# Marking the closing branch at the head of every paired loop of a four-layer graph kernel

## What is computed

```python
# layer 0: masked attention with 8 heads of 64
atts = einsum('hqk,hmk->hqm', x@Wq, x@Wk) / 8 - 1e16 * (1 - adj_or_eye)
out0 = einsum('hqm,hmk,hko->qo', softmax(atts), x@Wv, Wo)
# layer 1: relu((adj @ x) @ W.T + b)
# layer 2: edge attention; h = x @ edge_w; e = where(adj > 0, h @ h.T, -9e15)
out2 = adj * (softmax(x@node_w, axis=0) * softmax(e, axis=1)) @ (x@weight) + bias
# layer 3: relu((D^-1/2 (adj+I) D^-1/2 @ x) @ W.T + b)
```

## Time and profile before

| | us |
|---|---|
| median of three runs | 2666.68 |
| lowest, highest | 2665.36, 2668.89 |
| span of the profiled execution | 2664.4 |
| TensorE busy in it | 2511.2 |
| VectorE, ScalarE, GpSimd busy | 1549.8, 1364.3, 1134.1 |

### The profile page before, as it was taken

One profiled execution on the slowest core, in us unless ns is written; L12 is line 12 of the kernel. 1 busy time (PEld: TensorE's weight loads), 2 busy tenths in 40 slices (PEclk: granted clock), 3 DMA queues, 4 the chain that ended last, 5 costly groups with the idle time before them and its releaser, 6 DMA issues. The chain is left out here.

```text
span 2664.4 us, 67769 instructions
## 1 busy us (share of the span) xinstructions
PE 2511.2 (94%) x25068; PEld 1583.2 (59%) x25068; DVE 1549.8 (58%) x3014; ACT 1364.3 (51%) x2024; POOL 1134.1 (43%) x967
## 2 busy tenths in 40 slices
PE   7997999999999999999969998999999999979998
PEld 6885776767777777777734443774444444434443
DVE  3346887878878788778832222554545556633222
ACT  3336887877878778778823221323424334423221
POOL 0006887878778778778800222001111111110222
PEclk9998999999999999999989999999999999989999
DMA  3117999999999899999843564314556668543554
GB/s 131 63 56 154 188 179 162 189 168 172 174 167 176 161 177 177 162 172 186 150 125 101 203 207 147 107 36 129 153 164 164 178 178 219 145 136 100 203 201 142
DMA packets 777899, 412.88 MB, mean 155 GB/s; under 512 B 690656, under 2 KB 711904, under 8 KB 769248
## 3 DMA queue, kind: packets, MB, share of 16 engines
q1 hardware_dynamic: 777696, 409.82, 66.4%
HBM read 201.15 MB, written 38.44 MB: 90 GB/s over the span
## 5 line engine op out<-in xcount | busy, mean ns | idle before, releaser
L803 DVE CUSTOM_DVE_ANT_0 att_scores<-att_slots,att_adj 128x1024 f32<-128x1024 f32 x528 | 576.1, 1091 | 75.4 <-PE att_slots L667 33.7
L622 POOL TENSOR_TENSOR att_part_low<-att_scores,att_part_high 128x1024 f16<-128x1024 f32 x352 | 575.4, 1651 | 73.0 <-ACT att_part_high L787 61.7
L748 ACT ACTIVATE att_scores<-att_scores,att_nmax 128x1024 f32<-128x1024 f32 x528 | 551.9, 1046 | 23.5 <-DVE att_lifted L814 19.5
L667 PE MATMUL att_slots<-l_kk,att_q 128*128 128x512 f16 x2112 | 478.2, 363 | 48.8 <-issue 34.7
L1337 PE MATMUL a_ps<-l_y,a_adj 128*128 128x512 f16 (+1 forms) x1936 | 429.9, 381 | 9.0 <-DVE a_adj L1351 4.7
L757 ACT ACTIVATE att_near_high<-att_ps_t 128x512 f16<-128x512 f32 x528 | 258.5, 524 | 223.8 <-PE att_ps_t L678 220.4
L822 DVE TENSOR_TENSOR att_near_low<-att_ps_t,att_near_high 128x512 f16<-128x512 f32 x528 | 316.4, 599 | 66.1 <-ACT att_near_high L757 65.6
L1337 PEld LDWEIGHTS a_ps<-l_y,a_adj 128*128 128x128 f16 (+1 forms) x1936 | 182.6, 98 | 256.3 <-issue 40.2
L667 PEld LDWEIGHTS att_slots<-l_kk,att_q 128*128 128x128 f16 x2112 | 199.0, 100 | 213.2 <-issue 54.1
L1082 PE MATMUL edge_ps_o<-l_sup,edge_pt_high 128*128 128x512 f16 x968 | 288.1, 379 | 0.0
L1321 ACT ACTIVATE a_adj<-l_adj 128x2816 f16<-128x2816 f32 x44 | 112.0, 2550 | 298.4 <-DMA l_adj<-in_adj_cols 278.4
(11 more groups left out here) (149 smaller groups left out, 3865.0 us busy)
## 6 DMA issues: line engine op xcount, KB each, us to landing
l_adj<-in_adj_cols SPq DMA_DIRECT2D x44, 1408.0 KB, 6.2
l_adj_tiles<-in_adj SPq DMA_DIRECT2D x22, 1354.0 KB, 6.0
att_adj<-in_adj SPq DMA_DIRECT2D x66, 384.0 KB, 4.3
p_x_in<-x SPq DMA_DIRECT2D x66, 256.0 KB, 2.6
att_q<-q_rows SPq DMA_DIRECT2D x44, 256.0 KB, 3.8
a_xres<-x SPq DMA_DIRECT2D x44, 256.0 KB, 2.8
scores_rows<-edge_raw SPq DMA_DIRECT2D x8, 842.0 KB, 3.5
p_x_in<-in_x SPq DMA_DIRECT2D x22, 256.0 KB, 2.7
```

Source lines behind the costliest of these rows:

```text
L622: nc.gpsimd.tensor_tensor(out=part[1][:, v, lo:lo + width], in0=sc[:, v, lo:lo + width], in1=part[0][:, v, lo:lo + width], op=ALU.subtract ...
L667: mm = nc.tensor.matmul(slots[:, slot, z:z + w], q[:, u, h % 2, a, h // 2, :], kk[:, h, lo + z:lo + z + w], start=a == 0, stop=a == 1)
L748: nc.scalar.activation(sc[:, v, lo:lo + width], sc[:, v, lo:lo + width], ACT.Exp, bias=nmax[:, v:v + 1], scale=-1.0).then_inc(exp_done, 1)
L803: nc.vector.tensor_tensor_reduce(out=sc[:, v, lo:lo + width], in0=slots[:, (NC * h + c) % 2, 0:width], in1=adj[:, u, lo:lo + width], scale ...
```

## The change

`Fori` of one engine is replaced by `Fori` of the program with that one engine named and `hint_back_edge=True`. At the head of each turn the engine's sequencer now runs a branch hint that names the loop's closing compare-and-branch. Nothing else of a loop changes, and the hint comes on every engine that calls `pairs`, in every loop that has more than one turn.

```diff
-    with eng.Fori(0, turns) as i:
+    with eng.bass.Fori(0, turns, engines=(eng.engine,), hint_back_edge=True) as i:
         for t in (begin, begin + 1):
             step(i + t // 2, t % 2)
```

## The result

The changed kernel takes 2640.55 us (median of four runs, 2638.23 to 2643.20) against 2667.78 us (2665.36 to 2668.95) beside it: a ratio of 0.9905, 95% interval 0.9891 to 0.9919. It is 27.2 us faster. The forecast was 2611 us, 56.8 us faster, so the direction came and a little under half of the size did.

The account below looks back on a forecast made before the run. PE bounds the kernel, with attention's closing branches costing 57.8 us: 2664.4 - 57.8 + 0.8 + 1.6 = 2609.0 us, plus 2.3 for the median, forecast 2611 us. Its own range was 2607 to 2622, the overall range 2606 to 2662.

Parts of the forecast that it names:

- What bounds the kernel: PE, busy 94%; in attention eight taken closing branches cost 57.8 us, 34.7 idle and 23.1 at the lower clock.
- the second gap: PE's 0.48 us idle behind the eighth matmul of an attention turn, read as a second missing instruction block.
- (1): Hint on PE in attention: the branch falls to 208 ns, leaving 0.1 us each, 0.8 us in all.
- (2): Next late thing in attention, such as DMA transposes: 0.2 us for each of eight tiles, 1.6 us in all.
- A mechanism that keeps the hint in mind: Hint remembered until attention's closing branch comes near; the only escape from the hint doing nothing, and no row shows one.
- (3): The hint instruction's own time, 0 to 0.2 us a turn over PE's 63 taken turns: 0, at most 12.6 us.
- The cover: Other engines' hint time is hidden because PE is the busy one; without that, 0.1 us a turn.
- (4): Hints shift later code against block ends: costed at nothing if the target comes early.
- only the target is there: In attention the block behind the target comes late: 1.5 us idle a turn, 2621 to 2645 us; chance 0.15 with half hits.
- No effect: Hinted target overwritten before attention's branch, branches stay 4.1 us: 2667 us, or 2662 if shifted code helps; chance 0.15.
- Paid and not used: PE's ten loops pay 0.2 us in each of 63 taken turns, branches unchanged: 2679 us; chance 0.10.
- The signs: PE branches near 208 ns, no "issue" waits, attention turns 96 to 96.5 us at clock 1.00, other loops' turns unchanged.

Follow-up runs that it names:

- e5: Kernel before, no hint, only the head of PE's attention loop put at the start of a 256-instruction block: 2660.93 us, ratio 0.9986.
- e9: Kernel before plus plain hint on PE's attention loop, head at a block's start, hint between the body's two tiles: 2617.91 us, ratio 0.9821.
- e8: Kernel before plus register hint, not taken in the last turn, on every paired loop of every engine, PE's attention head at a block's start: 2616.93 us.
- e12: The changed kernel again, unaltered, on the third chip, against the kernel before: 2638.55 us, ratio 0.9897.
- e6: Kernel before plus plain hint on PE's attention loop alone, with its head at a block's start: 2618.19 us, ratio 0.9821.
- e7: Kernel before plus hint on PE's attention loop alone, from a register saying not taken in the last turn, head at a block's start: 2614.82 us.
- e11: Kernel before plus PE's attention loop with head at a block's start and register hint, plain hints on all other loops of all engines: 2624.32 us.
- e4: Kernel before plus plain hints on the loops of ScalarE, VectorE, GpSimd and SyncE, none on PE: 2676.19 us, ratio 1.0028.
- e1: Kernel before plus plain hint on PE's attention loop alone, its head left where it was: 2642.01 us, ratio 0.9902.
- e2: Kernel before plus plain hints on all loops except PE's in attention: 2688.61 us, ratio 1.0080.
- e10: Kernel before plus plain hint on PE's attention loop, head at a block's start, hint some 70 instructions ahead of the branch: 2662.86 us.

## Why the prediction was half right

- **What bounds the kernel.** Right: PE, and in attention the closing branch. e5 gives the second gap a price: alone it is worth 4.8 us by the medians, 3.7 by the ratio (the prediction's rivals had 5).
- **(1) and (2), the hint in attention.** Right in size: 825.9 - 771.2 = 54.7 us, where 57.8 - 0.8 - 1.6 = 55.4 were forecast. What is left are the 0.3 us gap and some 0.1 us a turn; the transposes were not late. The clock stayed at 1.00. The branch itself did not fall to the 208 ns of the other loops: it takes 0.5 to 0.65 us, and so 0.3 us of each show on the array where 0.1 were put, within the bound of 0.5. A mechanism that keeps the hint in mind, which no row could show, is what the chip has: e9 has it noted half a turn ahead.
- **(3), the price of the hint itself.** The instruction, 31 ns, is right at nothing: project 1, aggregate 1 and edge attention keep their turns of 6.05, 19.41 and 47.82 us, and e8 costs at most a few us with hints everywhere. But this part counted 63 taken branches of PE and left out those that aren't taken. That is the step that failed. A hint "taken" is wrong once per loop, and all ten loops of PE and those of four other engines have such an exit; I priced it at nothing. What was given back measured 30.4 us in the spans: 54.7 won in attention, 24.3 of it left. With the right outcome in the last turn, e8 gets back 23.6 us by the medians (21.6 against e12) with attention's turns at the same 771 us. By the outcome in the last turn alone (and the register operation that sets it), 3.4 us are shown at attention's exit on PE (e6 less e7) and 7.4 us at all the others (e11 less e8); the rest of the 30 us hangs on where the blocks lie, and on the spread of the runs.
- **The cover.** "The cover is PE" held for the hint, not for the exit. At a loop's end the next stage waits for VectorE, ScalarE, GpSimd and SyncE too, so their missing blocks (e4: 6.8 us, and 9 packets in q14 for 5) reach PE there, as waits for a semaphore, not as "issue". And a still PE brings the lower clock with it: in the edge stretch the granted clock is 0.93 against 1.00, with 2.9 us more of busy time for the same 214 matmuls behind 4.6 us of stillness.
- **(4), code that shifts.** Priced at nothing "if the target comes early, since the fetch of the second block can then overlap". Wrong by 21 us: e1, with the head where it was, loses 2.65 us a turn to the second block. The changed kernel escaped it because its head lies elsewhere (e6, with the head moved, has turns of 96.4 us). The rival "only the target is there" was right in kind for e1: its two gaps are 2.6 us where 1.5 were estimated. Its price stood between no loss of clock and the whole; e1 has none in seven of eight turns.
- **The rivals.** "No effect" fell. The Trainium skill ("Runtime: NRT & Kernel Launch", section "Instruction fetch mechanics") speaks of strictly sequential fetching and of a stall at a taken branch outside the instruction memory. The kernel before agrees, with branches of 4.1 us; with a hint this case doesn't, with 0.6 us and a fetch of the target 1.8 us ahead. The prediction took its window of two blocks of 256 instructions as PE's; the same section also gives PE 2048 instructions, which was left out. By that figure the 490 of the edge loop fit and the 2900 of attention don't, and the trace agrees: 12 to 14 fetches in a turn of attention, none while the edge loop turns at 47.82 us. "Paid and not used" fell as a cause too; e2 does come out slower, at 2688.61 us 10 us above its 2679, but as far as its profile shows by exits, not by the hint's time in turns.
- **The signs.** Turns of 96 to 96.5 us at clock 1.00 and unchanged turns elsewhere came as named, while half of the gain went. Two signs did not come: the branches take 0.5 to 0.65 us and not 208 ns, and "issue" stayed, with 2.4 us in attention's loop and 9.0 us in three new places. Those three lie between loops, the stretches that the list should have named.

## What to carry to other kernels

Hint a closing branch only where the body is longer than what the engine holds (here 2900 instructions, refetched in every turn; edge attention's loop, with some 490 matmuls and weight loads, gained nothing), put its head at a block's start, and let the hint say "not taken" in the last turn. That version, e7, takes 2614.82 us: 1.9% below the kernel before and 1.0% below the change. The right outcome alone is worth 3.4 us of it (e6 to e7). When an edit bets on one way of a branch, price the other way, for every engine and every loop that carries it, and read the windows between the loops.

## What the runs showed of the hardware

- The closing branch of attention's loop, whose target isn't held, takes 3.7 to 4.4 us on PE (before, e2, e4, e5, e10); hinted, 0.44 to 0.67. The hint takes 31 ns (VectorE 39).
- The hint fetches nothing when it is run. It replaces the next block in sequence by the target, in a fetch that starts some 1.8 us ahead of the branch and is settled earlier; 1450 instructions or 2900 make no difference (2617.91, 2618.19 us), 70 instructions, or 2.3 us, are too late (2662.86).
- A wrong "taken" can cost a block's fetch behind the exit: between nothing and 4.6 us of stillness on PE, and up to 3 us more through the clock.
- Where this loop's head lies in its block is worth about 4 us without a hint and 20 to 24 us with one (e6 against e1: 21.4 us in the turns).
- Left open: the median of e2, 11 us above its profiled run; why PE stands still for 2.3 us ahead of the late fetch in edge attention; and why a block missed by another engine shows in one stage and not in another.
